# Rotary embedding of queries and keys: the partner feature by a VectorE shuffle instead of a matrix product

## What is computed

```python
def rotate_half(x):
    d = x.shape[-1] // 2
    return jnp.concatenate([-x[..., d:], x[..., :d]], axis=-1)

def apply_rotary(q, k, position_ids, seq_len):
    ...
    return (q * cos + rotate_half(q) * sin, k * cos + rotate_half(k) * sin)
```

## Time and profile before

| | us |
|---|---|
| median of 3 runs | 3230.56 |
| lowest, highest | 3200.38, 3235.28 |
| profiled execution, its own time | 3209.79 |
| its span from the first to the last instruction | 3208.0 |
| PE busy | 2964.1 (92%) |
| DVE busy | 1617.9 (50%) |
| ACT busy | 1575.5 (49%) |
| POOL busy | 1018.6 (32%) |
| mean granted PE clock | 0.965 |

### The profile page before, as it was taken

How to read it: one execution, slowest core, us unless ns; L and a number is a source line. 1 busy time by engine, 2 the same in 40 slices (tenths; PEclk the granted TensorE clock), 3 DMA queues, 4 the chain that set the end, 5 groups by cost and what they waited for, 6 DMA issues and landing times.

```text
span 3208.0 us, 50404 instructions
## 1 busy us (share of the span) xinstructions
PE 2964.1 (92%) x16858; PEld 1705.2 (53%) x16858; DVE 1617.9 (50%) x3673; ACT 1575.5 (49%) x6978; POOL 1018.6 (32%) x998
## 2 busy tenths in 40 slices
PE   6999899998999999999999999999999999989998
PEld 4556455555555545555555554555556555455454
DVE  3435465565443445655554454665544345456554
ACT  2437355644343826555443472744634356364462
POOL 1014154342112415435211332443521033335341
PEclk9999999999999999989999999999999999999899
DMA  5010111102101011010210001101111000110111
GB/s 173 1 30 2 41 34 26 39 24 64 53 1 30 1 44 40 24 40 24 60 47 7 24 1 53 41 20 35 34 57 40 20 11 1 53 40 24 30 34 37
DMA packets 170980, 109.35 MB, mean 34 GB/s; under 512 B 31650, under 2 KB 168292, under 8 KB 170596
## 3 DMA queue, kind: packets, MB, share of 16 engines
q1 hardware_dynamic: 166272, 105.82, 11.6%
q10 hardware_dynamic: 4452, 0.29, 0.1%
HBM read 101.87 MB, written 4.19 MB: 33 GB/s over the span
## 4 chain that ended last, share of the span: by engine, by line
PE 71%; DVE 14%; ACT 11%; issue 3%; ACTq 1%; POOL 0%; DVEq 0%
PE proj L949 13%; ACT Ebuf L1370 8%; PE acc L1292 5%; PE pt_bank L1015 4%; PE proj L1226 4%; PE proj L1187 4%; PE acc L1196 3%; PE proj L954 3%; PE acc L1175 3%; PE scores L994 3%; PE proj L1168 3%; PE scores L1004 2%; PE o_bank L1031 2%; PE o_bank L1049 2%; PE scores L981 2%
## 5 line engine op out<-in xcount | busy, mean ns | idle before, releaser
L1370 ACT ACTIVATE Ebuf<-scores,minus_max 128x64 f32<-128x64 f32 x2592 | 772.3, 343 | 301.1 <-DVE minus_max L1564 299.5
L1746 POOL TENSOR_TENSOR Ebuf<-Ebuf,row_rcp 128x512 f32<-128x512 f32 (+1 forms) x328 | 343.1, 1047 | 1045.8 <-DVE row_rcp L1571 1045.0
L1370 ACT ACTIVATION_READ_ACCUMULATOR Ebuf<-scores,minus_max 128x1 f32 x2592 | 607.3, 237 | 0.0
L1564 DVE TENSOR_REDUCE minus_max<-scores 128x8 f32<-128x512 f32 (+1 forms) x328 | 221.4, 678 | 333.2 <-PE scores L981 129.7
L1379 ACT ACTIVATE PT<-pt_bank 128x512 f32<-128x512 f32 (+1 forms) x328 | 201.8, 615 | 143.2 <-PE pt_bank L1015 141.8
L1015 PE MATMUL pt_bank<-ident,Ebuf 128*128 128x128 f32 x1296 | 213.9, 288 | 12.1 <-POOL Ebuf L1746 11.4
L949 PE MATMUL proj<-xs_a,w_ring 128*128 128x512 f32 (+1 forms) x384 | 196.4, 636 | 2.9 <-DVE xs_a L1639 2.4
L1015 PEld LDWEIGHTS pt_bank<-ident,Ebuf 128*128 128x128 f32 x1296 | 147.3, 146 | 95.2 <-issue 73.3
L949 PE MATMUL proj<-xs_b,w_ring 128*128 128x512 f32 (+1 forms) x384 | 188.7, 615 | 7.0 <-DVE xs_b L1639 5.5
L1571 DVE RECIPROCAL row_rcp<-row_sum 128x8 f32<-128x8 f32 (+1 forms) x328 | 65.1, 199 | 237.1 <-ACT Ebuf L1370 236.3
L1792 POOL TENSOR_TENSOR arena_b<-arena_b,masks_b 128x384 f32<-128x384 f32 (+1 forms) x48 | 63.6, 1324 | 197.4 <-DVE arena_b L1716 197.4
(11 more groups left out here) (313 smaller groups left out, 6192.8 us busy)
## 6 DMA issues: line engine op xcount, KB each, us to landing
w_ring<-in_L_W SPq DMA_DIRECT2D x64, 256.0 KB, 3.1
w_ring<-in_L_l_gate SPq DMA_DIRECT2D x80, 128.0 KB, 2.2
w_ring<-in_L_l_up SPq DMA_DIRECT2D x80, 128.0 KB, 2.3
w_ring<-in_L_l_down SPq DMA_DIRECT2D x80, 128.0 KB, 2.2
w_ring<-in_L_v_gate SPq DMA_DIRECT2D x80, 128.0 KB, 2.4
w_ring<-in_L_v_up SPq DMA_DIRECT2D x80, 128.0 KB, 2.4
w_ring<-in_L_v_down SPq DMA_DIRECT2D x80, 128.0 KB, 2.5
arena_a<-in_x SPq DMA_DIRECT2D x4, 512.0 KB
```

Source lines behind the costliest of these rows:

```text
L1370: last = A(Ebuf[:, u % 3, cell], score_bank[u % 2][:, cell], ACT.Exp, bias=minus_max[:, u % 3, c:c + 1], accum_out=row_sum[:, u % 3, c:c + 1])
L1564: V.reduce_max(minus_max[:, u % 3, 0:g], cells(score_bank[u % 2][:, 0:g * S]), AX_X, negate=True).then_inc(maxed, 1)
L1746: G_.tensor_tensor(v, v, row_rcp[:, n % 3, 0:g].unsqueeze(2).broadcast_to([P, g, S]), ALU.mult).then_inc(probs_ready, 1)
```

## The change

The product with the matrix goes. In its place DVE moves each feature to its partner's partition with one `stream_shuffle` (a permutation within each group of 32 partitions, the same for the four groups), from `st.qk` to the scratch in `st.kbd`, waits for it (the new semaphore `turned`), and multiplies the scratch in place by the sines. The sign of the partner is put into the sine table once, at the start: PE sums the rows of the sign matrix, DVE takes the result as a column `turn_sign`, and multiplies the sines by it. POOL waits for the shuffle instead of for the product. "rot" is no longer a step of PE, so it leaves the list of bank users, and the planner's costs of "rot" and "table" are new.

```diff
+PARTNER = [p + HD // 2 if p % HD < HD // 2 else p - HD // 2 for p in range(32)]
...
-              "qk", "rot", "v", "cv", "ck", "cq", "dense", "cdense", "g", "u", "out")
+              "qk", "v", "cv", "ck", "cq", "dense", "cdense", "g", "u", "out")
...
     if step == "table":
-        return [("DVE", 3.0, None), ("PE", 0.3, 0), ("ACT", 0.3, None), ("POOL", 0.1, 0)]
+        return [("DVE", 3.3, None), ("PE", 0.4, 0), ("ACT", 0.3, None), ("POOL", 0.1, 0)]
     if step == "rot":
-        return [("PE", 0.93, None), ("DVE", 0.7, 0), ("POOL", 1.3, 0)]
+        return [("DVE", 1.35, None), ("POOL", 1.3, None)]
...
-BANK_FREE = {"g": 0.6, "sums": 0.3, "rot": 0.7}
+BANK_FREE = {"g": 0.6, "sums": 0.3}
...
@@ PE, table
-                        last.then_inc(s_table, 1)
-                        pe.wait_ge(s_table, 7)
+                        mm(acc[1][:, 0:1], rotate[:, :], ones[:, 0:1], start=True, stop=True).then_inc(s_table, 1)
+                        pe.wait_ge(s_table, 9)
...
@@ PE
-                    if step == "rot":
-                        n, i = where
-                        b = fill(token)
-                        pe.wait_ge(*qk_ready[s].at(turn, 4 * (n - 2) + i + 1))
-                        mm(b[:, :], rotate[:, :], st.qk[:, i, :], start=True, stop=True).then_inc(full(token), 1)
...
@@ DVE, table
-                    V.tensor_copy(cos_sin[:, :, :], acc[0][:, 0:2 * S].rearrange("p (a s) -> p a s", a=2)).then_inc(s_table, 1)
-                    dve.wait_ge(s_table, 7)
+                    V.tensor_copy(cos_sin[:, 0, :], acc[0][:, 0:S]).then_inc(s_table, 1)
+                    V.tensor_copy(turn_sign, acc[1][:, 0:1]).then_inc(s_table, 1)
+                    dve.wait_ge(s_table, 8)
+                    V.tensor_scalar(cos_sin[:, 1, :], acc[0][:, S:2 * S], turn_sign, None, ALU.mult).then_inc(s_table, 1)
+                    dve.wait_ge(s_table, 9)
...
@@ DVE, rot
-                    dve.wait_ge(*filled(token))
+                    k, v = 4 * (n - 2) + i, st.kbd[:, 1, i % 2, :]
+                    dve.wait_ge(*qk_ready[s].at(turn, k + 1))
                     if i >= 2:
-                        dve.wait_ge(*roped[s].at(turn, 4 * (n - 2) + i - 1))
-                    V.tensor_tensor(by_batch(st.kbd[:, 1, i % 2, :]), by_batch(bank(token)[:, :]),
+                        dve.wait_ge(*roped[s].at(turn, k - 1))
+                    V.stream_shuffle(v, st.qk[:, i, :], PARTNER).then_inc(turned[s].sem, 1)
+                    dve.wait_ge(*turned[s].at(turn, k + 1))
+                    V.tensor_tensor(by_batch(v), by_batch(v),
                                     cos_sin[:, 1, :].unsqueeze(1).broadcast_to([P, G, S]), ALU.mult).then_inc(sined[s].sem, 1)
...
@@ POOL, rot
-                    pool.wait_ge(*filled(token))
+                    pool.wait_ge(*turned[s].at(turn, 4 * (n - 2) + i + 1))
```

More of the change, by code:

```diff
@@ L629, in xattn_kernel @@
     early = small[:, 2:4]
+    turn_sign = small[:, 4:5]
     ident = sb("ident", [P, P])
@@ L730, in xattn_kernel @@
     wo_done, hid_ready, w2_done = pair("wo_done", JT), pair("hid_ready", NF), pair("w2_done", NF)
-    qk_ready, cosined, sined, roped = pair("qk_ready", 8), pair("cosined", 8), pair("sined", 8), pair("roped", 8)
+    qk_ready, turned, cosined, sined, roped = (pair(name, 8) for name in ("qk_ready", "turned", "cosined", "sined", "roped"))
     v_ready, kbd_by_dve, kbd_by_pool = pair("v_ready", 4), pair("kbd_by_dve", 16), pair("kbd_by_pool", 48)
@@ L776, in emptied @@
             return {"g": g_ready, "u": h_ready}[step][s].at(turn, FT * li + last + 1)
-        if step in ("qk", "rot"):
-            return {"qk": qk_ready, "rot": sined}[step][s].at(turn, 4 * li + last + 1)
+        if step == "qk":
+            return qk_ready[s].at(turn, 4 * li + last + 1)
         if step == "v":
@@ L1738, in _ @@
                 if step == "table":
-                    pool.wait_ge(s_table, 7)
+                    pool.wait_ge(s_table, 9)
                     pool.wait_ge(s_setup, 5)
```

## The result

The changed kernel takes 3130.97 us (median of 4 runs, 3125.79 to 3139.09), the one before 3222.38 us: a ratio of 0.9725 with an interval of 0.9663 to 0.9788. A repeat with five runs gave 3129.32 against 3227.02 us, 0.9700 (0.9678 to 0.9721). I take that one: 97 us less. I had forecast 3178 us, 41 us less, in a range of 3136 to 3222: faster, as said, but by more than twice what I had counted.

A forecast was written before the change was run, and what follows sets the result against it. PE was taken as the bound, with almost nothing to wait for at the rotary products and DVE half idle. 52.9 - 11 - 1 = 41 us less, from 3219 to 3178 us, range 3136 to 3222.

The forecast's parts named there:

- No mechanism, but a spread: each queue is planned anew: All queues: fillers and clock shift, about 23 us either way per hundredth of clock; chance of undoing the gain 0.04.
- The first term: PE in the rotary stages: 56 of 64 removed products on the chain, plus the wait for L1685, 52.9 us less.
- The second term: DVE's queue from shuffle to add: 79 us longer over 64 tiles, of which 11 us come on the path.
- The 14%: DVE's share of the chain over the whole span, taken as the part of its added time on the path.
- its 79 us: DVE's queue in the rotary stages: stands 1.24 us longer per tile, 79 us over 64 tiles.
- half is given back: Rival, layer 3: the longer DVE and POOL rotary chain takes over 25 us of the gain, 3203 us; chance 0.24.
- The larger gain through the early second scores: Rival: tile 3 needn't wait behind v 0, second scores come earlier, up to 28 us more, 3150 us; chance 0.16.
- Slower: Rival, after each stage's first shuffle: DVE's queue becomes the bound, 3298 us, or 3246 in mild form; chance 0.11.
- Shuffle: forecast 0.69 with 0.16 for a load: DVE, each tile: shuffle at 0.69 us plus 0.16 for a possible permutation load, 54.4 us over 64.
- the pair 0.69 and 1.70: DVE and POOL after the shuffle: if DVE goes first, sine product takes 0.69 us and POOL's L1769 1.70.
- My reading that it speaks against the change: DVE and POOL port pair: exclusive lock makes the later one stand, add starts 1.70 to 1.83 us after shuffle.
- One of my own signs of being wrong: Whole kernel, profile after: the forecast is wrong if the mean clock moves by over 0.01.

The follow-up runs named there:

- Kernel 2: Changed instructions in the queue order of the kernel before, the product left out of PE's queue: 1.0006 to the kernel before, 3228.11 us.
- kernel 9: Changed instructions, planner keeps the product as a PE step (left out afterwards) but counts DVE's shuffle and product at 1.35 us: 0.9903 to the kernel before.
- 10: Changed kernel, planned without the product on PE but with DVE's part at the old 0.7 us instead of 1.35: 0.9790 to the kernel before.
- 1: The changed kernel once more, unaltered, against the kernel before: 0.9700, 3129.32 us.
- 4: Changed kernel, tile 3's shuffle allowed only after PE's first value projection, queues planned anew: 0.9727 to the kernel before.
- 11: Changed kernel, planned with the trace's times, DVE 1.45 us and POOL 2.5 us: 0.9664 to the kernel before, 3115.97 us.
- kernel 6: Kernel before, product still on PE, in the queue order of the changed kernel: 0.9946 to the kernel before.
- kernel 12: Kernel before with each rotary product made twice into its bank, same queues: 1.0099 to the kernel before.
- kernel 3: Changed kernel with 64 products of the same size put back on PE and overwritten, no wait of their own: 0.9829 to the kernel before.
- kernel 8: Changed kernel with each shuffle made twice, same queues: 0.9921 to the kernel before.
- kernel 5: Kernel 2 with tile 3's rotary work on DVE and POOL moved before the first self attention scores' maximum and normalisation: 1.0091 to the kernel before.
- kernel 15: Changed kernel, 28 times in DVE's queue the next tile's shuffle put ahead of the add: 0.9732 to the kernel before, 3128.70 us.
- 7: Kernel before with the planner's PE cost of the product set to 0.86 us for 0.93: 0.9970 to the kernel before.

## Why the prediction was wrong

**The step that failed** is the last of the rivals, "No mechanism, but a spread: each queue is planned anew", which I priced at 23 us either way; my sum had no term for it at all. The new plan has a sign. Kernel 2 shows that the same instructions in the old queues gain nothing, where I had summed 41 us; kernels 9 and 10 that the two costs which the change tells the planner are worth 31 and 68 us. The mechanism of the 31 us is shown: 12 times DVE no longer sits idle before a reciprocal with tile 3 behind it. That of the rest is not. I had treated the diff of the cost table as bookkeeping. That the new plan is good by chance isn't excluded by a kernel of its own, but the four plans made without the product gave 0.966 to 0.979 (kernels 1, 4, 10 and 11), and the new queues gave the old instructions nothing at equal clock (kernel 6).

**The first term, 52.9 us for PE's products,** is near the price of a product but not what its removal gives. I counted links of the chain that ended last, 56 at 0.86 us. At equal clock, adding a product to each tile costs 45 us in the old order (kernel 12) and 38 us in the new one (kernel 3). Taking it away while the order stands gives nothing, with DVE's longer work in its place (kernel 2), and one path that comes up at once is tile 3 behind the reciprocal (kernels 2 and 9). With the queues planned for its absence the span of the profiled executions fell by about as much as all of PE's work for the products, 66.6 us, more than the chain had shown.

**The second term, 11 us for DVE's wait, was too small for a fixed order.** The 14% was a share of the whole span; in the place itself about all of the added DVE time is on the path at equal clock. That was measured in the new order (kernel 8). For the old order no run adds DVE time alone; but if PE gives some 45 us there and nothing remains, the longer rotary chain took about that much of its 79 us. My rival "half is given back" named that mechanism, but for layer 3 alone, and had its extent wrong. For the kernel as changed, the plan puts the value projections ahead of the first scores in 12 of 16 stages; that this is what hides DVE's work fits the traces, but no run isolates it.

**The larger gain through the early second scores** was some 9 us, not clear of noise (kernel 4). **Slower** didn't come: it would have needed DVE's time unhidden in the new order, which kernel 8 shows one step on, still 0.8% under the kernel before.

**The sizes of the parts held.** Shuffle: forecast 0.69 with 0.16 for a load, measured 0.72 with 0.014. Sine product and POOL: the pair 0.69 and 1.70 was forecast for DVE going first, measured 0.69 and 1.77, and POOL never went first on stream a. The time from shuffle to the end of the add: 3.34 forecast, 3.37 measured (406.50 to 409.87 us). The rule of the Trainium skill ("SBUF — State Buffer", SBUF: two separate sides) that VectorE work with two SBUF inputs and GpSimd work that reads SBUF exclude each other fits POOL's 1774 ns, 502 more than the 1272 before. My reading that it speaks against the change was wrong as a forecast of the time. The estimate from its shuffle figure ("VectorE: DVE Perf Modes", the perf-mode tier table), 0.80 us, was 11% above the 0.72 measured.

**The level.** The clock of the typical run is part of the effect: 0.959 before, 0.970 after, about 25 us by the slope, with an execution at 0.965 as my base. I had named the clock as a spread and not asked in which direction a new plan would move it. One of my own signs of being wrong, a mean clock that moves by over 0.01, came true in the medians.

**What adds up.** From the kernel before to the changed one in three steps: new order with the old product 17 us (kernel 6), the product and its bank taken out of the rotary chain but its time left on PE 38 us (6 to 3), its time taken off PE 42 us (3 to 1); 97 us together. At equal clock the three are about 2, 34 and 38 us, and the rest is the clock. The first two lean on where kernel 6 puts the product, which costs it some waits of its own. Of the moved steps one is identified, the first reciprocal behind tile 3, 31 us (kernel 9 against kernel 2); putting tile 3 before the maximum instead (kernel 5) or exchanging neighbours in the new order (kernel 15) gave nothing. Open remains which steps carry the other two thirds.

## What to carry to other kernels

Where the order of the queues is computed from a table of costs, a change of an instruction is two changes, and each needs its own run: the new instruction in the old queues, and the new queues. A link count in the chain that ended last can come near the price of doubling the link (48 and 45 us here) and still not be the gain from removing it, when several paths run side by side; one kernel with the cost doubled tells the price, one with the link gone and the order kept the gain. Compare the queues of two plans before you say that they differ, or that they don't: a changed cost moved 12 steps in one kernel here (7), and the few steps that it moved in another (9) named the place that was worth 31 us. And tell the planner the time that the new trace shows: here the median fell by another 13 us, though the intervals overlap.

## What the hardware showed unasked

- The clock answers to small changes of the order: medians from 0.949 (kernel 5) to 0.972 (kernel 15) with nearly the same instructions, at some 23 us for 0.01. Without the 260 and 253 fillers, 83 and 72 us of PE work that computes nothing, it fell to 0.934 and 0.939 and the kernels were 1.6 and 2.0% slower.
- Where DVE and POOL were released by the same event, POOL's instruction was the one that grew: on stream a all 32 cosine products took 1770 to 1782 ns, and the sine product never more than 694.
- The load of the shuffle's table took 14 ns and lies inside the shuffle's own 0.72 us; the shuffle over 128 partitions by 512 float32 costs 4% more than an add of that size.
